# Expert rows in a tensor of their own, filled in 8 KB stretches, and a new set of leads for the planner

## The reference

```
x = x + L0_xattn(layernorm(x), ctx)     # Q + causal(K K^T) Q, without softmax
x = x + L0_ffn(layernorm(x))            # latent attention (16 heads of 8), then 8 experts of width 512, top 2
x = x + L1_xattn(layernorm(x), ctx)     # cross attention, 16 heads of 64, output projection, tanh gate
x = x + L1_ffn(layernorm(x))            # 16 experts of width 256, top 2, and a shared expert of width 512
```

## Time and profile before

| | |
|---|---|
| median of 3 runs | 990.42 us (988.06 to 992.68) |
| profiled execution | 989.18 us |
| its span, first to last instruction | 987.4 us |
| TensorE matmul busy | 910.0 us, 92% |
| VectorE busy | 723.1 us, 73% |
| ScalarE busy | 611.7 us, 62% |
| GpSimd busy | 293.6 us, 30% |
| HBM read, written | 62.24 MB, 46.00 MB |
| granted TensorE clock, mean | 0.98 |

### The profile page before, as it was taken

The page is one execution under the profiler, slowest core; times in us unless marked ns, Lnnn a source line. Parts: engine busy times, 40 slices in busy tenths (PEclk is TensorE's granted clock), DMA queues, the critical chain, the costliest instruction groups (busy, mean ns, idle before and its releaser), DMA issues.

```text
span 987.4 us, 24585 instructions
## 1 busy us (share of the span) xinstructions
PE 910.0 (92%) x8304; PEld 813.8 (82%) x8304; DVE 723.1 (73%) x1957; ACT 611.7 (62%) x1694; POOL 293.6 (30%) x375
## 2 busy tenths in 40 slices
PE   4899889887999999998799999999998999898997
PEld 3776666654999999997699888998987988898896
DVE  5768788776676667674889978977876637776757
ACT  3487767773666666675577657786775236665640
POOL 3855666763000000001642435311212003232320
PEclk9899999998999999999799999999999999999999
DMA  8549999201131111113110132030028813232235
GB/s 293 160 161 300 352 245 253 56 29 55 53 137 55 49 51 53 55 34 117 43 35 12 33 98 76 23 98 23 23 65 352 290 44 87 77 90 85 82 114 190
DMA packets 59563, 109.82 MB, mean 111 GB/s; under 512 B 6225, under 2 KB 46033, under 8 KB 58033
## 3 DMA queue, kind: packets, MB, share of 16 engines
q1 hardware_dynamic: 52576, 89.42, 29.6%
q0 software_dynamic: 6864, 18.85, 5.7%
HBM read 62.24 MB, written 46.00 MB: 110 GB/s over the span
## 4 chain that ended last, share of the span: by engine, by line
PE 61%; issue 13%; DVE 9%; DMA 8%; POOL 5%; ACT 2%; SPq 0%; DVEq 0%; POOLq 0%; ACTq 0%
PE ps L888 15%; PE ps L718 8%; PE ps L720 8%; PE ps L719 8%; POOL yt_dram L1962 4%; PE ps L975 3%; DMA xs_dram<-zero 3%; PE ps L985 3%; PE ps L999 3%; PE ps L1057 2%; DMA kv_dram<-BIG 2%; PE ps L786 1%; PE ps L824 1%; PE ps L810 1%; ACT BIG L1151 1%
## 5 line engine op out<-in xcount | busy, mean ns | idle before, releaser
L718 PE MATMUL ps<-BIGR 128*128 128x256 f32 (+1 forms) x826 | 260.5, 315 | 6.5 <-DVE BIGR L1797 2.2
L888 PE MATMUL ps<-BIG 128*128 128x128 f32 x2000 | 253.8, 276 | 11.3 <-DVE BIG L1683 10.2
L888 PEld LDWEIGHTS ps<-BIG 128*128 128x128 f32 x2000 | 238.0, 192 | 15.4 <-DVE BIG L1683 13.1
L720 PE MATMUL ps<-BIGR 128*128 128x256 f32 x778 | 222.3, 286 | 0.0
L719 PE MATMUL ps<-BIGR 128*128 128x256 f32 (+1 forms) x602 | 179.2, 298 | 0.0
L718 PEld LDWEIGHTS ps<-BIGR 128*128 128x128 f32 x826 | 159.3, 193 | 14.4 <-issue 7.5
L720 PEld LDWEIGHTS ps<-BIGR 128*128 128x128 f32 x778 | 148.6, 191 | 0.7
L1197 ACT COPY BIG<-BIG 128x512 f32 (+1 forms) x86 | 70.1, 815 | 100.8 <-PE ps L888 87.2
L719 PEld LDWEIGHTS ps<-BIGR 128*128 128x128 f32 x602 | 116.3, 193 | 2.1 <-issue 0.3
L1676 DVE TENSOR_TENSOR BIGR<-BIG,BIGR 128x512 fp32r<-128x512 f32 (+1 forms) x86 | 80.3, 934 | 34.5 <-ACT BIGR L1206 34.3
L1954 POOL DMA_INDIRECT BIG<-ys_dram,YI x32 | 32.5, 1016 | 232.5 <-DMA ys_dram<-BIG 224.3
(11 more groups left out here) (234 smaller groups left out, 1916.5 us busy)
## 6 DMA issues: line engine op xcount, KB each, us to landing
xs_dram<-zero SPq DMA_DIRECT2D x17, 1024.0 KB, 19.5
BIG<-in_wgu SPq DMA_DIRECT2D x2, 6144.0 KB, 19.1
BIG<-in_wd SPq DMA_DIRECT2D x2, 4096.0 KB, 22.1
BIG<-xs_dram SPq DMA_DIRECT2D x47, 129.5 KB
BIG<-xs_dram SPq DMA_DIRECT2D x39, 128.0 KB
ys_dram<-BIG SPq DMA_DIRECT2D x39, 128.0 KB, 1.7
BIG<-in_wkv SPq DMA_DIRECT2D x2, 2048.0 KB, 9.9
kv_dram<-BIG SPq DMA_DIRECT2D x16, 256.0 KB, 4.1
```

The lines of the kernel that those rows point to most:

```text
L718: pe.matmul(o, l[0], r[0], start=start, stop=False)
L720: return pe.matmul(o, l[1], r[0], start=False, stop=stop)
L888: i = pe.matmul(o[:, c * 128:(c + 1) * 128], wt[:, at:at + 128], x[:, k * 128:(k + 1) * 128], start=k == 0, stop=k == 1)
```

## The change

1. The rows of the first experts get a DRAM tensor of their own, `XS0`, with rows of 256 numbers that follow each other. Scatters and reads of the first round use it, and the scatters write 256 numbers instead of 259. The second round no longer waits for the reads of the first one.
2. The fill is cut into 16 transfers in 8 groups of two. One transfer writes 136 rows of each expert in 17 pieces of 8 KB. Its source is the context in on-chip memory, of which eight partitions (every sixteenth) give 8 KB each, repeated 17 times; the values don't matter, only that they are finite.
3. Groups 0 and 1 wait for the context's loads alone; group g from 2 on waits for `tt` of sequence 2g-4. In the plan they follow `stats1` of sequence 4, or that `tt`.
4. `LEAD` has new values for many steps.

```diff
-BLANK = [range(2 * g, 2 * g + 2) for g in range(7)] + [range(14, 17)]
+BLANK = [range(2 * g, 2 * g + 2) for g in range(8)]
...
-    "EC": -100, "ET": -200, "K": 100, "K_e": -700, "PV": -100, "Q_e": 200, "SD": 400, "V": 100, "V_e": -100,
-    "W": 100, "ah": -300, "al": -200, "btg": 1800, "c_e": -1700, "ch": 900, "cl": -700, "cnt": -100, "cpow": 1000,
-    "ctxh": -800, "ctxl": -1600, "ep1": -4200, "epow": -1400, "exp0": 200, "exp1": 300, "ga0": 4300,
-    "gates_a": -2300, "hnT": -300, "kmh": -100, "kvwl": -100, "kw": 600, "log": -100, "max3": -100, "nl": 200,
-    "ow": -300, "owl": 1200, "pT3": 100, "pT_e0": 400, "pow2": -1000, "pow3": 200, "pro1": 400, "pro2": -900,
-    "pv": -100, "qkT": -200, "qkv": -300, "qw": -200, "r": 100, "rope": -300, "rope_p": -100, "route1": 2400,
-    "sc1": 1100, "stats1": 800, "swh": 500, "swl": 600, "vw": 1100, "wx": 200, "xbt": 1300, "xf": -300, "xh": 700,
-    "xl": -3000, "xr": 1400
+    "EL": -200, "ET": -200, "K": 100, "K_e": -600, "PV": -300, "Q_e": 200, "SD": 400, "SG": 200, "V": 100,
+    "V_e": -200, "W": 100, "ah": -300, "al": -200, "btg": 2900, "c_e": -1700, "ch": 900, "cpow": 900, "ctxh": -800,
+    "ctxl": -1600, "exp0": 200, "exp1": 300, "ga0": 4500, "hnT": -300, "kmh": -100, "kvwl": -100, "kwl": 800,
+    "load_kv": 3200, "load_q": 2800, "log": -100, "max3": -100, "nl": 200, "owl": 1100, "pT3": 100, "pT_e0": 400,
+    "pow2": -1000, "pow3": 200, "pro1": 400, "pro2": -2800, "pv": -100, "qkT": -200, "qkv": -300, "qw": -700,
+    "r": 100, "ra1": -300, "rope": -300, "rope_p": -100, "sc1": 1200, "sm": -800, "ss": 1600, "stats1": 800,
+    "swh": 300, "swl": 500, "vw": 1700, "wx": 200, "xbt": 900, "xf": -200, "xh": 1500, "xl": -1600, "xr": 1400
...
-        p.add("SP", 120, ("blank", g), ("tt", g - 1) if g else ("kmh", 0), late=4000)
+        p.add("SP", 120, ("blank", g), ("tt", 2 * g - 4) if g >= 2 else ("stats1", 4), late=3000)
...
+        XS0 = nc.dram_tensor("xs0_dram", [E0 * CAP, D], F32, kind="Internal").ap()
...
-                if g:
-                    sp.wait_ge(*done("tt", g - 1))
-                    if g >= 3:
-                        sp.wait_ge(sem(f"cleared{g % 3}"), 16 * sum(len(BLANK[k]) for k in range(g % 3, g, 3)))
+                if g < 2:
+                    sp.wait_ge(sem("ct_loaded1"), 16 * (NB // 2 - 2 - len(EARLY_KV)))
+                    sp.wait_ge(sem("ct_loaded2"), 16 * len(EARLY_KV))
                 else:
-                    sp.wait_ge(*done("kmh", 0))
-                    sp.wait_ge(sem("zeroed"), 1)
+                    sp.wait_ge(*done("tt", 2 * g - 4))
+                if g >= 3:
+                    sp.wait_ge(sem(f"cleared{g % 3}"), 16 * sum(len(BLANK[k]) for k in range(g % 3, g, 3)))
                 for c in BLANK[g]:
-                    sp.dma_start(XS[0:E0 * CAP, 0:D].rearrange("(e c) n -> c e n", c=CAP)[128 * c:128 * c + 128],
-                                 zero[:, 0:D].rearrange("p (o n) -> p o n", o=1).broadcast_to([128, E0, D])
+                    rows = CAP // 16
+                    sp.dma_start(XS0.rearrange("(e s k r) n -> s e k (r n)", e=E0, s=16, k=rows // 8)[c],
+                                 CT[c:128:16, NB // 2:NB, :, :].rearrange("p b k t -> p (b k t)")
+                                 .rearrange("p (o n) -> p o n", o=1).broadcast_to([E0, rows // 8, 8 * D])
                                  ).then_inc(sem(f"cleared{g % 3}"), 16)
```

More of the change, by code:

```diff
@@ L1936, in sc @@
                             pool.wait_ge(sem(f"cleared{g % 3}"), 16 * sum(len(BLANK[k]) for k in range(g % 3, g + 1, 3)))
-                if r and b == 0:
-                    for i in range(3):
-                        pool.wait_ge(sem(f"rows_loaded{i}"), 16 * len(range(i, NT0, 3)))
                 for k in range(2):
-                    pool.indirect_dma_start(XS, bass.IndirectOffsetOnAxis(ap=PI[:, b, k:k + 1], axis=0),
-                                            TT[tile_of(r, b)][:, :], None).then_inc(sem(f"scattered{tile_of(r, b)}"), 16)
+                    pool.indirect_dma_start(XS if r else XS0, bass.IndirectOffsetOnAxis(ap=PI[:, b, k:k + 1], axis=0),
+                                            TT[tile_of(r, b)][:, 0:ROW if r else D], None
+                                            ).then_inc(sem(f"scattered{tile_of(r, b)}"), 16)
             def ga(r, b):
@@ L2030, in pad_sp @@
                 sp.wait_ge(sem("zeroed"), 7)
-                for i in range(3):
-                    sp.wait_ge(sem(f"rows_loaded{i}"), 16 * len(range(i, NT0, 3)))
                 for x in range(E1):
@@ L2053, in xs @@
                         sp.wait_ge(*done("ix", 1, j - 3))
-                sp.dma_start(XS_[r][j % 3], XS[bass.ds(at, 128), 0:ROW if r else D]).then_inc(sem(f"rows_loaded{j % 3}"), 16)
+                sp.dma_start(XS_[r][j % 3], (XS if r else XS0)[bass.ds(at, 128), :]).then_inc(sem(f"rows_loaded{j % 3}"), 16)
             def ys(r, j):
```

## The result

The changed kernel takes 1014.81 us (median of 4 runs, 1013.16 to 1017.58), the kernel before 989.24 us beside it (984.59 to 992.68): a ratio of 1.026, 95% interval 1.021 to 1.032. It is 2.6% slower, where 1% faster was forecast. The profiled execution has a span of 1011.6 us, 24.2 us more than before.

A forecast was written before the change was run, and what follows sets the result against it. TensorE, busy 910 of 987 us, left room only in the latent stage and at the seams. Terms -1 - 3.5 - 5 - 0.5 = -10 took 989.2 to 979.2, as a median 980.5 us; forecast range 972 to 985 (0.60), outer ends 971.5 and 994.

The forecast's parts named there:

- Part 1: First four fills, issued at about 22 us: 5.5 us each, ACT's sixth kv copy earlier, minus 1 us.
- Rival A: First four fills block the kv stores at 9.2 us each: copy 14 us late, sum +5, 995.6 us; chance 0.16.
- Part 2: Later fills in the latent stage: GpSimd's two scatter waits for fills go, minus 3.5 us, ends 0 and minus 6.2.
- Part 3: Seam to cross attention: last expert store ahead of wq and wo loads, minus 5.0 us, ends minus 3 and minus 7.5.
- Rival D: Store still goes behind the loads in the new plan, so the seam gains 0: 985.5 us; chance 0.06.
- Part 4: Other leads, in cross attention and route of the second experts: minus 0.5 us, ends plus 5 and minus 5.
- B: DMA waits of the latent stage were slack; only the seam's minus 5 stays, 985.4 us; chance 0.08.
- C: New order in the cross attention costs as much as the seam gives, +5: 986 us; chance 0.10.

The follow-up runs named there:

- shapes A and H, B and I: Fills in a kernel without computation, from eight partitions: 16 apart in 8 KB (11.4 us) and 2 KB pieces (11.7); 4 apart in 8 KB (5.7) and 2 KB (5.9).
- e_paths: Changed kernel with fills read from partitions 4 apart instead of 16 apart; 971.15 us against 982.68 for the kernel before, ratio 0.989.
- e_front: Changed kernel with only the first four fills read from partitions 4 apart, the later twelve 16 apart; 990.29 against 984.46 us, ratio 1.005.
- after: The changed kernel, with new fills and new leads; 1014.81 us against 989.24 for the kernel before, ratio 1.026.
- before: The kernel without the change; 989.24 us beside the changed kernel.
- e_loadq: Kernel before with one lead added, load_q +2800, so the last store precedes the loads of wq and wo; 985.38 against 984.46 us, ratio 0.998.
- e_leads: Kernel before with the whole new LEAD table and its old fills; 974.52 against 982.68 us, ratio 0.993.
- e_leads2: Repeat of the kernel before with the new LEAD table and old fills; 984.57 against 987.37 us, ratio 0.997.
- e_paths2: Repeat of the changed kernel with fills from partitions 4 apart; 977.14 against 987.37 us for the kernel before, ratio 0.989.
- shapes D and E: Fills in a kernel without computation, 128 partitions, 1 KB pieces: rows 1036 B apart as before (4.6 us a transfer) and 1024 B apart (3.4).

## Why the prediction was wrong

**Part 1 failed in one term, the price of a fill.** It took 5.5 us (201 GB/s) with 9.2 us as the slow end; the chip took 11.4 us (100 GB/s), outside both ends. The number of engines was right: eight, a share of 0.50. The rate of each was taken from weight loads, 25.1 GB/s, with the fill of 1 KB pieces as the floor, 15.2. From partitions 4 apart the estimate would have been right to 0.2 us (5.7 us measured). Both rows came from transfers over all 128 partitions, though; the step left out that the new source touches only eight, and which eight. The bound "from both sides" was no bound, because the new transfer differed from both rows in a thing that neither showed. A row could not have settled it. The index `c:128:16` in the diff was the place to ask the question.

**Rival A is what happened, and larger.** Its mechanism holds: the first four fills keep the kv stores behind them, and ACT's copies wait. Its price does not: 9.2 us came from the rate of 1 KB pieces, and between 2 and 8 KB the length made no difference for these sources (shapes A and H, B and I). With 11.4 us in its own sum, the fills end at 21.3 + 4 x 11.4 = 67 and the store behind them lands by 70, where ACT goes on at 70.27. Rival A had 59 and 60. It counted the delay of the copy in full, and that is nearly so: the fifth copy is 28.9 us late, the scatter of sequence 0 25.5. The front thus cost 25 us instead of 14.

**Part 2 failed in the words "in time in either case".** The waits at sequences 2 and 4 went, as forecast, and two others came. The prediction gave each fill the time since its own release (over 45 us), as if each pair had the engines to itself. But group 3 was not issued at its release. It stands behind the last weight load of the first experts, 6 MB that itself waits for the kv stores (the last of them landed when it was issued, at 135.77; in e_paths it goes out at 100.83), and the fills go out at 136.21. The load fills the engines until about 151 (share 0.92 in 137 to 150); two fills then take 23 us, to 174. The scatter of sequence 6 waits until 176.16. From there ten fills are a queue of their own: 151 + 10 x 11.4 = 265, and the scatter of sequence 14 waits until 267.16. At 5.7 us the same ten would be over by 208, and in e_paths no scatter waits. The prediction's sum held minus 3.5; measured it is plus 10.9, or plus 10 to 12 by e_front. What it missed was the total: 16 fills of 11.4 us are 182 us of a stage of 241.

**Part 3 was right in the order and wrong in what the order moves.** The store goes ahead of the loads, and in after the gather follows 2.15 us behind the issue of wq, instead of 8.36:

```profile
490.93 0.43 SPq L2104 DMA_DIRECT2D BIG<-in_wq  x1
```

```profile
493.08 0.98 POOL L1952 DMA_INDIRECT BIG<-ys_dram,YI  x1 [218.76 <-DMA ys_dram<-BIG]
```

```profile
504.09 0.45 PE L1020 MATMUL ps<-CS,BIG 128*128 128x128 f32 x1 [2.74 <-DVE BIG L1757]
```

The first scores are 5.3 us nearer to that issue than before, which is the minus 5.0 of the sum, but luck has a part in it. The step that failed is that DVE's run of results "moves with the gather": by e_loadq the gather went 5.7 us earlier and DVE started 2.4 us earlier, since the gathered rows took 7.3 us instead of 4.1 beside the two loads. The prediction let the loads hold up the store and nothing else. The transposes gained 3.1 us, and the other 2.1 came from the slow clock, which the prediction had only as an extra of up to 2.5. In after TensorE's gap fell from 4.89 to 2.74 us and not below 1, and the clock still was 0.50 from 504 to 506 us. The step also stopped at the first products: of 5.2 us in e_loadq 2.7 were left at the last scores, and two pairs of kernels that differ in SP's order alone show a gain of 0.2% (interval minus 0.1 to 0.5) and of nothing. Rival D, that the plan would not do it, is out.

**Part 4** held minus 0.5 us, ends 5 either way. The new leads as a whole measured 0.7% and 0.3% faster in two rounds (7 and 3 us) with fills of before. With `load_q` worth 0 to 2 of it, the rest lies in the part that was put down as a wash. In after, the cross attention took 3.0 us longer between its first and last scores, the limit that the prediction had set; in e_leads it took the same 252 us as before. That is no finding, though: e_leads2, the same kernel as e_leads, took 255.4 us. `route` came 5.2 us sooner after the last scores, and 3.9 of that was lost again before the first result was stored. So what can be told of the size lies near or within its ends; where the leads gain, the runs don't tell.

**Rivals B and C.** B held that fills and waits were slack. For the first four fills it is refuted: they cost 25 us. For the two waits of the earlier trace rows the runs don't decide. With the waits gone, e_paths ends the latent stage at 234.69 and e_paths2 at 236.93, before at 235.65, and e_leads and e_leads2 with the old fills at 233.05 and 238.04; a gain of 3.5 us would be hidden in that spread. The medians put e_paths 3.4 and 7.4 us under e_leads, which is against B, but don't say that these waits are the reason. C (a new order that costs as much as the seam gives) is not what happened.

Added up in the profiled executions: +25.5 for the front, +10.9 for the later fills, -5.3 at the seam, +3.0 and -1.3 in the cross attention and the second seam, -9.2 in the second experts: +24 us (with 0.6 more between the latent stage and the seam).

## What to carry to other kernels

A transfer between on-chip memory and DRAM is priced by three things: how many DMA engines its outer dimension gives it, how many of the shared paths its partitions reach, and only then the length of its pieces. Eight partitions 16 apart reached 100 GB/s, eight neighbours 55, and eight partitions 4 apart 213, so a wide spacing is no sign of many paths. The profile shows the narrow case as a DMA share of one half at a quarter of the bandwidth or less. Whoever moves filler traffic ahead of stores that free buffers should sum it over the whole queue, not transfer by transfer: what is harmless at 5.7 us each was 36 us at 11.4.

## What the runs showed beyond that

**Rows 12 B further apart cost a third.** 1 KB pieces from 128 partitions took 4.6 us a transfer (229 GB/s) at 1036 B from row to row, and 3.4 us (338 GB/s) at 1024 B: shapes D and E, which are also in different tensors. The prediction counted the 12 B as nothing. The rates are those of a window within each; the time of a transfer also holds the start and the landing of each group of four:

```profile
170.00:174.00 4.00, 0.00 (x0) 0.00 (x0) 1.00 1.13 229
186.00:190.00 4.00, 0.00 (x0) 0.00 (x0) 1.00 1.04 338
```

**The second experts differ between executions of one order.** After and e_paths have the same instructions there, yet the stage takes 134.4 us in one and 141.9 in the other (143.6 before). DVE (L1629) waits for the landing of a scatter four tiles back; that wait in 800 to 990 us, first before, then after:

```profile
DVE PL L1629 <- DMA yt_dram<-BIG,IX: 29.5, 20, 3.1
```

```profile
DVE PL L1629 <- DMA yt_dram<-BIG,IX: 18.9, 18, 1.6
```

The longest wait was 3.1 us before and 1.6 after. Two pairs show that this comes without the change: e_leads and e_leads2 are one kernel, and their stages take 142.7 and 134.6 us, with waits of 28.6 and 18.0 in total; e_paths and e_paths2 take 141.8 and 134.3, with 28.5 and 16.1. Of the thirteen profiled executions seven have 27.9 to 32.4 us of this wait and a stage of 141.1 to 143.9 us, and six have 16.1 to 21.3 us and 134.3 to 139.1. The 9.2 us that after seems to gain there are therefore not put down to the change. In both pairs the cross attention goes the other way (252.0 and 255.4 us in e_leads and e_leads2, 252.2 and 257.2 in e_paths and e_paths2). Over all its runs the kernel before took from 976 to 996 us. That the landing times make the spread is argued from the waits that go with it; no run tested it, and why they differ is open.
